# A graph layer with two expert choices per node: keys summed on VectorE, 16-bit marks of the choices' places, last rows stored in two pieces

## The chip, the cores and the metric

The kernel runs on one core of one Trainium2 chip. The metric is the device time of one execution in microseconds (us). TensorE (PE in the profile, PEld its weight loads), VectorE (DVE), ScalarE (ACT), GpSimd (POOL) and SyncE (SP, which here only issues transfers) run their own instruction streams side by side and wait for one another by semaphores. Matrix products end in PSUM, all other tiles lie in SBUF.

## The reference, cut to what matters

```python
xn = layernorm(x)                                    # x: [3125, 256]
# gnn: 53125 edges, sorted by dst
agg = segment_sum(edge_weight[:, None] * xn[src], dst, 3125);  gnn = agg @ W.T + b
# mix: linear attention, 8 heads
Q, K = elu(xn @ Wq) + 1, elu(xn @ Wk) + 1;  v = (xn @ Wv) / L
KV = einsum('nshd,nshv->nhdv', K, v)
Z = 1 / (einsum('nlhd,nhd->nlh', Q, K.sum(axis=1)) + 1e-6)      # the keys summed over tokens
mix = xn + layernorm(relu([xn, layernorm((Q KV Z L) @ Wm)] @ W1) @ W2)
x = x + gnn + mix
# ffn: 16 experts, the two best of each node, hidden size 512
n3 = layernorm(x);  top_probs, top_idx = top_k(softmax(n3 @ gate_w + gate_b), 2)
x = x + sum over the two choices of  gate * (silu(n3 @ w1[e]) * (n3 @ w2[e])) @ w3[e]
```

## The kernel before

The 3125 rows are 25 tiles of 128 tokens (NT = 25), of which the last has 53 rows (LAST). All is float32 but for a few bf16 marks. The stages follow each other:

1. **Load and normalise** (to about 42 us). x is loaded, normalised to xn, turned by TensorE, and the messages' rows y = xn @ W.T are made and stored to memory.
2. **Keys** (about 43 to 122 us). For t in 0..24 `project_k(t)` makes the key projection (L721); ScalarE (`exp_keys`, L417 and L419) and VectorE (`keys`, L1154) make the elu; three tiles later `sum_xk(t)` adds xn.T @ keys into one PSUM bank (L739) and, by a matmul of each key block with one column of ones (L742), the sum of the keys over the tokens into two columns of another. `xk_added` counts the tiles; GpSimd's gathers and SyncE's loads wait on it. Beside this the first two of 13 groups of edges are sorted: VectorE counts and places (`find_places`: L1054 to L1073, after TensorE's `prefix`, L683 to L686) and makes records (L1086, L1094), ScalarE makes one-hot marks of the slots (`slot_hot`, L382 and L384, four for each group), and TensorE puts a group in order by `reorder` (L695, 16 matmuls, four for each group). TensorE's order is written by hand: `reorder(0, k)` in tile steps 4, 6, 8 and 10, `prefix(1)` in step 17, `reorder(1, k)` in steps 22, 23, 25 and 27. ScalarE's: `slot_hot(0, k)` after tiles 1, 3, 5 and 7, `slot_hot(1, k)` after tiles 19, 20, 22 and 24. VectorE's is a list of `keys(first, end)` calls with the sort's parts between them. After the last `reorder`, `make_list(1)` (L1108 to L1132) and register loads on VectorE (`bins_named`) end the stage.
3. **Sums over edges** (about 124 to 840 us). 13 groups of 56 steps. GpSimd gathers 32 tiles of rows for each group (L633), ScalarE scales them, TensorE meets them with one-hot marks (L902, L912), VectorE adds into agg (L1212, L1218). The attention's and the next sort's parts are placed by hand beside the steps.
4. **Gate and routing** (about 840 to 922 us). n3 is made and stored (L313, and L314 for the last 53 rows), logits, the two choices, and for each choice its slot in the experts' list of 64 tiles (ETILES) of 128 places. `slots_ready` lets SyncE load the first experts' weights. Then the token of each place is found: VectorE marks the tile (`in_etile`, [P, 2, 25, 64] bf16) and the place in the tile (`in_place`, [P, 2, 25, 128] bf16) of each choice from int32 slots and a float32 iota (L1507), ScalarE multiplies `in_etile` by the row number (L559), GpSimd by the tile number (L645), and TensorE sums over tokens (L955). For each choice it waits for all three. VectorE turns the sums into token indices (L1511 to L1524, `tokens_ready`), GpSimd gathers the tokens' rows (L650).
5. **Experts** (about 926 to 1285 us). 64 tiles in a loop: 32 matmuls up (L978), 8 down (L988), three weight loads of 512 KB by SyncE for each, one gather and one scatter by GpSimd.
6. **End.** SyncE loads both choices' rows back, VectorE adds them with the gates, SyncE stores the output: four transfers of five tiles, one of four tiles (L361), one of the last 53 rows (L362), and waits for all.

## Time and profile before

| | |
|---|---|
| median of 3 runs | 1322.45 us (1321.16 to 1322.45) |
| the profiled execution | 1325.14 us, span in the profile 1323.4 us |
| busy PE / PEld / DVE / ACT / POOL | 1148.7 / 1016.0 / 850.8 / 537.1 / 621.3 us |
| mean granted TensorE clock | 0.939 of full |
| chain that ended last, by engine | PE 54%, DVE 21%, VectorE's queue 10%, issue 8%, ACT 3%, DMA 2% |

A busy share is an average over six stages with different limits. For each edit the row that counts is that of its own stage: who is waited for last there. The profiled execution is 1.7 us longer than its span and 2.7 us longer than the median.

### The profile page before, as it was taken

What the parts mean: (1) busy time and instruction counts of PE and PEld (TensorE: products, weight loads), DVE (VectorE), ACT (ScalarE), POOL (GpSimd) and SP (SyncE); (2) the same over time, 40 slices, a digit from 0 to 9 for tenths busy, and PEclk for the clock granted to TensorE, in tenths of its full rate; (3) what the DMA queues carried; (4) which work ended last, traced back from release to release, by engine and by line L of the source; (5) the groups of instructions that cost most, each with busy time, mean ns of one, the idle gap of its engine ahead of it and who ended that gap; (6) DMA issues with size and microseconds to landing.
All of it is one profiled execution on the core that took longest, in us unless ns stands there. A gap on an engine that the chain in (4) does not pass through costs nothing.

```text
span 1323.4 us, 21724 instructions
## 1 busy us (share of the span) xinstructions
PE 1148.7 (87%) x6831; PEld 1016.0 (77%) x6831; DVE 850.8 (64%) x1960; ACT 537.1 (41%) x1247; POOL 621.3 (47%) x624
## 2 busy tenths in 40 slices
PE   6998798999989899898998998741999999999980
PEld 5897686787868778687786886641999999999970
DVE  8644788888888888988889877857222222222226
ACT  4747575573856648466483742211011111111100
POOL 5845447566575755657566471004233333333320
PEclk9899899999999999999999999755999999999995
DMA  7213123222222222222222231205699999999948
GB/s 208 82 55 109 54 63 93 68 82 71 72 80 68 89 66 83 72 68 84 68 85 72 64 97 32 79 19 178 232 331 332 327 340 333 335 327 336 329 158 284
DMA packets 118372, 196.12 MB, mean 148 GB/s; under 512 B 13526, under 2 KB 67604, under 8 KB 118292
## 3 DMA queue, kind: packets, MB, share of 16 engines
q1 hardware_dynamic: 88958, 120.62, 27.5%
q0 software_dynamic: 26112, 71.34, 17.1%
q10 hardware_dynamic: 3222, 3.20, 0.7%
q8 instruction: 37, 0.61, 0.2%
q14 instruction: 43, 0.35, 0.1%
HBM read 177.12 MB, written 17.99 MB: 147 GB/s over the span
## 4 chain that ended last, share of the span: by engine, by line
PE 54%; DVE 21%; DVEq 10%; issue 8%; ACT 3%; DMA 2%; SPq 1%; ACTq 0%; POOL 0%; POOLq 0%
PE psum L978 17%; PE psum L988 8%; PE psum L902 6%; DVE agg L1212 5%; DVE agg L1218 4%; PE psum L912 3%; PE psum L721 3%; PE psum L695 3%; PE psum L789 2%; PE psum L739 2%; ACT in_slot L382 2%; PE psum L841 2%; DVE hot L1205 2%; DVEq L1297 1%; DVEq L1085 1%
## 5 line engine op out<-in xcount | busy, mean ns | idle before, releaser
L633 POOL DMA_INDIRECT arena<-y_rows,gather_i x416 | 440.6, 1059 | 301.6 <-PE psum L902 121.1
L902 PE MATMUL psum<-arena,hot 128*128 128x256 f32 x832 | 222.6, 397 | 15.9 <-DVE hot L1205 6.7
L1212 DVE TENSOR_TENSOR agg<-psum,agg 128x256 f32 x416 | 174.5, 420 | 44.8 <-DVE agg L1212 20.9
L479 ACT ACTIVATE arena<-arena,listed 128x256 f32<-128x256 f32 x416 | 175.6, 498 | 65.6 <-DMA arena<-y_rows,gather_i 65.5
L902 PEld LDWEIGHTS psum<-arena,hot 128*128 128x128 f32 x832 | 151.4, 195 | 53.1 <-issue 23.8
L978 PEld LDWEIGHTS psum<-arena 128*128 128x128 f32 x1536 | 181.4, 194 | 4.9 <-issue 2.5
L978 PE MATMUL psum<-arena 128*128 128x128 f32 x1536 | 181.9, 277 | 2.0 <-DVE arena L1531 2.0
L1538 DVE TENSOR_TENSOR arena<-psum,arena 128x512 f32<-128x512 f32 x64 | 44.3, 692 | 204.9 <-PE psum L978 204.9
L569 ACT ACTIVATE arena<-psum 128x512 f32<-128x512 f32 x64 | 38.3, 598 | 335.1 <-PE psum L978 335.1
L655 POOL DMA_INDIRECT chosen_rows<-arena,back_at x64 | 63.4, 990 | 219.7 <-DVE arena L1545 215.0
L382 ACT ACTIVATE in_slot<-iota,place_f 128x128 f32<-128x128 f32 x416 | 127.3, 390 | 62.2 <-DVE place_f L1073 62.0
L912 PE MATMUL psum<-arena,hot 128*128 x624 | 150.9, 382 | 1.5 <-DVE agg L1218 0.6
L912 PEld LDWEIGHTS psum<-arena,hot 128*128 128x128 f32 x624 | 115.5, 192 | 17.9 <-issue 3.7
L1218 DVE TENSOR_TENSOR agg<-psum,agg 128x512 f32<-128x512 f32 x156 | 106.0, 679 | 24.0 <-PE psum L912 22.4
L695 PE MATMUL psum<-record,in_slot 128*128 128x96 f32 x832 | 101.8, 275 | 0.0
L695 PEld LDWEIGHTS psum<-record,in_slot 128*128 128x128 f32 x832 | 99.5, 192 | 2.3
L988 PE MATMUL psum<-arena 128*128 128x256 f32 x384 | 90.8, 379 | 0.0
L650 POOL DMA_INDIRECT xnT<-n_rows,token_of x64 | 62.2, 972 | 28.4 <-issue 18.9
L988 PEld LDWEIGHTS psum<-arena 128*128 128x128 f32 x384 | 69.2, 190 | 7.4
L1094 DVE TENSOR_TENSOR record<-in_tile,edge 128x256 f32<-128x256 f32 x156 | 68.4, 447 | 5.5
L1545 DVE COPY arena<-psum 128x256 f32<-128x256 f32 x64 | 27.2, 425 | 60.7 <-PE psum L988 60.7
L1205 DVE TENSOR_TENSOR hot<-iota,node_in_bin 128x1024 f32<-128x1024 f32 x52 | 63.4, 1219 | 3.4 <-issue 2.5
(208 smaller groups left out, 1662.4 us busy)
## 6 DMA issues: line engine op xcount, KB each, us to landing
arena<-in_L_ffn_w_dram SPq DMA_DIRECT2D x144, 512.0 KB, 5.6
xnT<-in_L_ffn_w_dram SPq DMA_DIRECT2D x48, 512.0 KB
arena<-y_rows,gather_i POOLq DMA_INDIRECT x416, 2.8
arena<-chosen_rows SPq DMA_DIRECT2D x8, 640.0 KB, 8.9
y_rows<-w ACTq DMA_DIRECT2D x6, 512.0 KB, 2.9
agg<-in_x_dram SPq DMA_DIRECT2D x4, 640.0 KB, 6.7
n_rows<-arena SPq DMA_DIRECT2D x4, 640.0 KB
out_dram<-agg SPq DMA_DIRECT2D x4, 640.0 KB
```

The source lines that it names most:

```text
L382: act.activation(in_slot[k % 2][:, c, :], iota[:, :], ACT.Abs, bias=place_f[:, k * CH + c:k * CH + c + 1])
L479: last = act.activation(rows[h][:, t, :], rows[h][:, t, :], ACT.Copy, scale=weight[h][:, t:t + 1])
L633: pool.indirect_dma_start(rows[h][:, t, :], None, y_rows, bass.IndirectOffsetOnAxis(ap=gather_i[h][:, t:t + 1], axis=0)).then_inc(gathered ...
L695: last = pe.matmul(in_order, in_slot[k % 2][:, c, :], record[k % 2][:, c, :, :].rearrange("p f t -> p (f t)"), start=(k == 0 and c == 0), ...
L902: pe.matmul(bank_of(g, t // 2)[:, (t % 2) * C:(t % 2 + 1) * C], hot[:, n % HOTS, :], rows[h][:, t, :], start=True, stop=True).then_inc(met, 1)
L912: pe.matmul(bank_of(g, unit)[:, (b % 2) * C:(b % 2 + 1) * C], hot[:, n % HOTS, :], rows[h][:, bass.ds(row_of[b], 1), :].rearrange("p t c - ...
L978: last = pe.matmul(bank[b][:, m * P:(m + 1) * P], w[s][:, k * EH + m * P:k * EH + (m + 1) * P], e_xT[:, h, k * P:(k + 1) * P], start=(k == ...
L988: last = pe.matmul(bank[6 + h][:, 0:C], e_hid[:, h, k * P:(k + 1) * P], e_w3[s][:, k * C:(k + 1) * C], start=(k == 0), stop=(k == EHC - 1))
L1094: last = dve.tensor_tensor(record[k % 2][:, :, f, :], in_tile[:, :, :], edges_of(edge[:, f, :], g, k).unsqueeze(2).to_broadcast([P, CH, GT ...
L1205: dve.tensor_tensor(hot[:, n % HOTS:n % HOTS + BATCH, :], iota[:, :].unsqueeze(1).to_broadcast([P, BATCH, P]), of.unsqueeze(2).to_broadcas ...
L1212: dve.tensor_tensor(own, bank_of(g, t // 2)[:, (t % 2) * C:(t % 2 + 1) * C], own, ALU.add).then_inc(evicted, 1)
L1218: dve.tensor_tensor(own, bank_of(g, GT // 2 + a), own, ALU.add).then_inc(evicted, 1)
```

## The change

Four edits:

- The matmuls with ones leave `sum_xk`. VectorE adds each tile of keys to `keys_sum` ([P, 256] float32) instead: `sum_keys(t - 1)` comes right behind the key tile t, with a drain before it (26 instructions in all: a copy and 24 adds, with two of them behind the last tile). At the end of the keys stage TensorE waits for `keys_summed` and makes the two sums over partitions by one matmul each with ones. SyncE's load of Wm and W2, which overwrites the key tiles, waits for it as well.
- The slots' parts are copied to bf16, each value twice in a row (`slot_twice`, 200 elements from 100). The marks compare bf16 with bf16 (`iota_b`), in runs of two elements.
- GpSimd's multiplication by the tile number moves to VectorE (`number_tiles`), in the same form, between the marks: both `in_etile`, a drain, then for each choice the numbered tiles and `in_place`.
- The last 53 rows of n3 and of the output are stored as 48 rows and 5 rows.

```diff
+    ROUND = LAST // 16 * 16
...
                 for k in range(KC):
-                    pe.matmul(bank[5][:, k * C:(k + 1) * C], xn[0:tokens, t, k * P:(k + 1) * P], keys_of[0:tokens, t % 4, :],
-                              start=(t == 0 and k == 0), stop=(t == NT - 1), skip_group_check=True)
-                for m in range(KC):
-                    last = pe.matmul(bank[6][:, m:m + 1], keys_of[0:tokens, t % 4, m * P:(m + 1) * P], ones[0:tokens, 0:1],
-                                     start=(t == 0 and m == 0), stop=(t == NT - 1), skip_group_check=True)
+                    last = pe.matmul(bank[5][:, k * C:(k + 1) * C], xn[0:tokens, t, k * P:(k + 1) * P], keys_of[0:tokens, t % 4, :],
+                                     start=(t == 0 and k == 0), stop=(t == NT - 1), skip_group_check=True)
                 last.then_inc(xk_added, 1)
...
+            pe.wait_ge(keys_summed, 1)
+            for m in range(KC):
+                pe.matmul(bank[6][:, m:m + 1], keys_sum[:, m * P:(m + 1) * P], ones[:, 0:1], start=True, stop=True)
...
+            def sum_keys(t):
+                dve.drain()
+                if t == 0:
+                    return dve.tensor_copy(keys_sum[:, :], keys_of[:, 0, :])
+                n = P if t < NT - 1 else LAST
+                return dve.tensor_tensor(keys_sum[0:n, :], keys_sum[0:n, :], keys_of[0:n, t % 4, :], ALU.add)
...
                     dve.scalar_tensor_tensor(keys_of[:, t % 4, :], bank[t % 4][:, 0:C], 0.0, k_neg[:, t % KC, :], ALU.max, ALU.add).then_inc(k_ready, 1)
+                    if t >= 1:
+                        sum_keys(t - 1)
+                    if t == NT - 1:
+                        sum_keys(t).then_inc(keys_summed, 1)
...
-            for c in range(2):
-                pool.wait_ge(etiles_made, c + 1)
-                pool.tensor_tensor(numbered[:, c, :, 1, :], in_etile[:, c, :, :],
-                                   token[:, :, 1 + c].unsqueeze(2).to_broadcast([P, NT, ETILES]), ALU.mult).then_inc(tile_numbers, 1)
...
+            dve.tensor_copy(slot_twice[:, :, :, :, :].rearrange("p a c t b -> p (a c t) b"),
+                            slot_parts[:, :, :, :].rearrange("p a c t -> p (a c t)").unsqueeze(2).to_broadcast([P, 4 * NT, 2]))
+            dve.drain()
+            def by_twos(a, n):
+                return a.rearrange("p t (s b) -> p t s b", b=2), [P, NT, n // 2, 2]
+
+            def mark_choice(to, part, c, n, done):
+                to, whole = by_twos(to[:, c, :, :], n)
+                dve.tensor_tensor(to, slot_twice[:, part, c, :, :].unsqueeze(2).to_broadcast(whole),
+                                  iota_b[:, 0:n].rearrange("p (s b) -> p s b", b=2).unsqueeze(1).to_broadcast(whole), ALU.is_equal)\
+                    .then_inc(done, 1)
+
+            def number_tiles(c):
+                to, whole = by_twos(numbered[:, c, :, 1, :], ETILES)
+                dve.tensor_tensor(to, by_twos(in_etile[:, c, :, :], ETILES)[0], tile_twice[:, c, :, :].unsqueeze(2).to_broadcast(whole),
+                                  ALU.mult).then_inc(tile_numbers, 1)
+
+            for c in range(2):
+                mark_choice(in_etile, 1, c, ETILES, etiles_made)
+            dve.drain()
+            for c in range(2):
+                number_tiles(c)
+                mark_choice(in_place, 0, c, P, places_made)
...
-                    sp.dma_start(out[(NT - 1) * P:N, :], agg[0:LAST, NT - 1, :]).then_inc(out_written, 16)
+                    for first, end in ((0, ROUND), (ROUND, LAST)):
+                        sp.dma_start(out[(NT - 1) * P + first:(NT - 1) * P + end, :], agg[first:end, NT - 1, :]).then_inc(out_written, 16)
```

The store of n3's last rows (L314) is split in the same way, and the waits on `n3_stored` and `out_written` count one transfer more.

## Rows read from the trace of the kernel before

**Rows 1.** Windows: busy us (instructions) of each engine, then clock, DMA share, GB/s.
```profile
49.00:76.00 27.00, 27.00 (x156) 24.63 (x157) 13.66 (x26) 20.01 (x54) 11.06 (x15) 0.88 0.11 38
...
98.00:122.00 24.00, 24.00 (x162) 22.51 (x161) 9.82 (x32) 20.35 (x53) 17.49 (x19) 1.00 0.42 131
...
900.00:922.00 22.00, 5.91 (x50) 5.15 (x50) 17.48 (x14) 4.54 (x3) 11.15 (x3) 0.57 0.61 215
922.00:1285.00 363.00, 356.61 (x2688) 342.51 (x2688) 92.67 (x192) 38.28 (x64) 123.94 (x127) 0.99 0.91 310
```

**Rows 2.** Timeline of TensorE, one key tile: start us, us, instructions [idle before].
```profile
80.20 0.50 PE L742 MATMUL psum<-ones,w 128*128 128x1 f32 x4
...
80.56 1.11 PE L721 MATMUL psum<-wky,xnT 128*128 128x256 f32 x4
...
81.51 1.03 PE L739 MATMUL psum<-w,arena 128*128 128x256 f32 x4
...
82.37 0.50 PE L742 MATMUL psum<-ones,w 128*128 128x1 f32 x4
```

**Rows 3.** Timeline of ScalarE in the first sort, two waits for TensorE.
```profile
58.96 0.39 ACT L417 ACTIVATE wm<-psum 128x256 f32<-128x256 f32 x1 [1.01 <-PE psum L721]
...
65.09 0.39 ACT L417 ACTIVATE wm<-psum 128x256 f32<-128x256 f32 x1 [1.04 <-PE psum L721]
```

**Rows 4.** Timeline of the second sort, from its prefix to its list.
```profile
92.76 0.99 DVE L1054 SCALAR_TENSOR_TENSOR count<-psum,count 128x800 f32<-128x800 f32 x1 [0.59 <-PE psum L686]
...
97.27 2.46 ACT L382 ACTIVATE in_slot<-iota,place_f 128x128 f32<-128x128 f32 x8 [0.41 <-DVE place_f L1073]
...
114.14 1.06 ACT L384 ACTIVATE in_slot<-in_slot 128x1024 f32<-128x1024 f32 x1
...
117.75 2.02 PE L695 MATMUL psum<-record,in_slot 128*128 128x96 f32 x16
...
119.88 0.19 DVE L1108 CAST gather_i<-psum 128x32 int32<-128x32 f32 x1 [6.57 <-PE psum L695]
```

**Rows 5.** Timeline of VectorE, the same three instructions twice.
```profile
50.20 2.52 DVE L1094 TENSOR_TENSOR record<-in_tile,edge 128x256 f32<-128x256 f32 x3
...
60.88 1.10 DVE L1094 TENSOR_TENSOR record<-in_tile,edge 128x256 f32<-128x256 f32 x3
```

**Rows 6.** Timeline of GpSimd, first and last gather of group 0.
```profile
79.43 1.39 POOL L633 DMA_INDIRECT arena<-y_rows,gather_i  x1 [19.22 <-PE psum L742]
...
120.03 0.95 POOL L633 DMA_INDIRECT arena<-y_rows,gather_i  x1 [0.30 <-issue]
```

**Rows 7.** Timeline of the routing's last part.
```profile
900.17 3.56 DVE L1507 TENSOR_TENSOR xnT<-slot_parts,iota 128x1600 bf16<-128x1600 int32 x2
...
902.09 10.51 POOL L645 TENSOR_TENSOR xnT<-xnT,token 128x1600 bf16<-128x1600 bf16 x2 [99.69 <-DVE xnT L1507]
903.65 12.29 DVE L1507 TENSOR_TENSOR arena<-slot_parts,iota 128x3200 bf16<-128x3200 int32 x2
...
909.89 2.95 PE L955 MATMUL psum<-xnT,arena 128*128 128x128 bf16 x25 [20.08 <-DVE arena L1507]
...
916.00 2.95 PE L955 MATMUL psum<-xnT,arena 128*128 128x128 bf16 x25 [3.15 <-DVE arena L1507]
...
918.99 0.23 DVE L1511 TENSOR_SCALAR token_tile<-psum 128x64 f32<-128x64 f32 x1 [3.05 <-PE psum L955]
...
925.95 0.66 PE L966 MATMUL psum<-ident,xnT 128*128 128x128 f32 x2 [7.00 <-DMA xnT<-n_rows,token_of]
```

**Rows 8.** Chain of waits: 32 up matmuls of an early and a later expert tile.
```profile
927.32 6.34 PE psum L978 x32
935.12 3.81 PE psum L978 x32
```

**Rows 9.** Waits of SyncE: what for, us in total, times, longest.
```profile
SPq L317 <- DVEq L1499: 31.5, 1, 31.5
...
SPq L68 <- DMA out_dram<-agg: 5.2, 1, 5.2
```

**Rows 10.** End: issue of the last store; GB/s from 1285 us, in slices of 0.975 us.
```profile
1317.38 0.36 SPq L362 DMA_DIRECT2D out_dram<-agg  x1
...
GB/s 134 29 105 1 68 356 355 367 362 356 347 350 349 348 346 353 345 350 348 350 347 348 339 351 379 233 335 348 335 350 350 122 24 105 351 121 24 24 14 0
```

More of the change, by code:

```diff
@@ L303, in _ @@
             sp.wait_ge(xk_added, NT)
+            sp.wait_ge(keys_summed, 1)
             sp.dma_start(wm[:, :, :], Wm.rearrange(chunks, p=P)).then_inc(late_weights, 16)
@@ L313, in _ @@
                     sp.dma_start(n3_tiles[:, i * U:NT - 1, :], n3[:, i * U:NT - 1, :]).then_inc(n3_stored, 16)
[L314 removed]
+                    for first, end in ((0, ROUND), (ROUND, LAST)):
+                        sp.dma_start(n3_rows[(NT - 1) * P + first:(NT - 1) * P + end, :], n3[first:end, NT - 1, :]).then_inc(n3_stored, 16)
             def e_owner(q, s):
@@ L361, in _ @@
                     sp.dma_start(out_tiles[:, i * U:NT - 1, :], agg[:, i * U:NT - 1, :]).then_inc(out_written, 16)
-                    sp.dma_start(out[(NT - 1) * P:N, :], agg[0:LAST, NT - 1, :]).then_inc(out_written, 16)
-            sp.wait_ge(out_written, 16 * (TURNS + 1))
+                    for first, end in ((0, ROUND), (ROUND, LAST)):
+                        sp.dma_start(out[(NT - 1) * P + first:(NT - 1) * P + end, :], agg[first:end, NT - 1, :]).then_inc(out_written, 16)
+            sp.wait_ge(out_written, 16 * (TURNS + 2))
         @block.scalar
@@ L1504, in _ @@
             dve.drain()
-            for part, to, n, done in ((1, in_etile, ETILES, etiles_made), (0, in_place, P, places_made)):
-                for c in range(2):
-                    dve.tensor_tensor(to[:, c, :, :], slot_parts[:, part, c, :].unsqueeze(2).to_broadcast([P, NT, n]),
-                                      iota[:, 0:n].unsqueeze(1).to_broadcast([P, NT, n]), ALU.is_equal).then_inc(done, 1)
+            dve.tensor_copy(slot_twice[:, :, :, :, :].rearrange("p a c t b -> p (a c t) b"),
[18 more added lines that the diff above has]
+                mark_choice(in_place, 0, c, P, places_made)
             dve.wait_ge(tokens_summed, 1)
```

20 lines of the change are left out of this document (12 added, 8 removed).

## The prediction

> **What bounds the kernel now.** I read the page first (busy shares and the chain by line), then windows by stage, then the timeline of the stages that the diff touches, and for the end SyncE's waits and the transfers' rate. No single engine bounds the kernel, so each edit is costed in its own stage [rows 1]. In the keys stage TensorE is busy without a gap: 27.00 of 27.00 us and 24.00 of 24.00 us, VectorE only 13.66 and 9.82. ScalarE is the one to watch there, 20.35 of 24.00 us at the end of the stage. In the window of the routing's last part nothing but VectorE's marks is long: they run from 900.17 to 915.9 us and TensorE waits for them twice [rows 7]. The expert loop is TensorE's again, 356.61 of 363.00 us, with the transfers at a share of 0.91 close behind [rows 1]. At the end the program waits 5.2 us for the last store [rows 9]. Nothing in the diff touches the sums over edges or the expert loop, so a shift won ahead of them should pass through them whole, unless something that starts earlier now lacks its input; I come to that below.
>
> **The keys: what goes.** One tile takes TensorE 2.17 us, from 80.20 to 82.37 [rows 2]. The four matmuls with ones cost 0.36 us of it (80.20 to 80.56). The four of L721 behind them take 0.95 us to L739's start, where the four of L739, with as much work, take 0.86 (81.51 to 82.37): another 0.09 us goes with the weight loads for the short ones. I take 0.44 us for each tile. 25 tiles make 11.0 us; the first two ran at a lower clock (the window from 49 us has a mean of 0.88 [rows 1]), for which I add 0.5 us. TensorE alone would finish the stage 11.5 us earlier.
>
> **Does something else become the bound?** First sort: two tiles and one `reorder` make a period of 6.13 us (58.96 to 65.09), in which ScalarE idles 1.04 us [rows 3]. ScalarE's own work is thus 5.09 us, and TensorE's new period 6.13 - 0.88 = 5.25 us. TensorE stays the bound, just. 15 tiles' ones lie ahead of `prefix(1)`, so it comes 15 x 0.44 + 0.5 = 7.1 us earlier. Second sort: from here ScalarE sets the pace. `find_places` takes 4.51 us (92.76 to 97.27), and ScalarE's four `slot_hot` with the keys between them run without a gap from 97.27 to 114.14 + 1.06 = 115.20 us, 17.93 us [rows 4]. Before, TensorE came to the last `reorder` only at 117.75, 2.55 us after its marks. Now `find_places` starts at 92.76 - 7.1 = 85.7 us, plus 0.3 because the add behind key 17 stands in front of it and the prefix is now there sooner: 86.0. Then 86.0 + 4.5 + 17.9 + 0.1 of latency = 108.5 us for the last `reorder` against 117.75: 9.2 us. So of TensorE's 11.5 us some 2.3 stay behind a wait for ScalarE.
>
> **What VectorE's 26 instructions cost.** Three instructions of 256 elements take 1.10 us where GpSimd does not compute, 0.34 us from start to start with 0.08 us behind the last; beside GpSimd's adds, up to some 60 us, the same three take 2.52 us [rows 5]. With the drain I take 0.42 us each, 11 us in all, and up to 0.9 us each for the first four. VectorE has 13 us free in the first window and 14 in the last. They lie behind the key tile that TensorE waits for, but in front of the sort's records: two adds for each `make_records`, some 0.9 us. The first records were ready three to five us before their `reorder`, except the second set (made at 54 to 58 us, beside GpSimd's adds), where I expect the slack to be used up: 0.3 us lost. The whole edit is then worth 9.2 - 0.3 = **8.9 us**. Its bounds: 11.5 if ScalarE's run shrinks too; 4.5 if the adds also delay the records of the second sort by 0.9 us in each of four sets and the contended ones cost another 1 us. The two pairs of matmuls with ones at the end (0.4 us) and the wait for `keys_summed` (VectorE's last adds end about 1 us before the last `reorder`) stand behind that `reorder`, where TensorE has two us before the first marks of the sums are made; nothing for them. SyncE's load of Wm and W2 is queued behind the same wait, is needed some 20 us later, and comes earlier than before. If the adds' cover were gone, they would cost their 11 us and eat the gain.
>
> **The shift's inputs.** GpSimd's 32 gathers of group 0 run back to back from 79.43 to about 121 us [rows 6], and their first waits for tile 9, which comes 4 us earlier. They end near 117 us, while the sums now begin near 115 instead of 124. The sums take their tiles in order over 55 us, and the first four tiles are there by 84 us, so this holds. Group 1's first gather slips to 117 from the 113 it could have had; it has 50 us. Nothing lost.
>
> **The marks.** Two instructions of 1600 elements start at 900.17 and leave the engine to the next at 903.65: 1.74 us each [rows 7]. With 0.34 us for 256 elements [rows 5] that is 0.07 us and 1.04 ns for each element; 3200 elements should take 3.41 us. They took 6.1 (903.65 to 915.94 for two), while GpSimd's multiplication stood beside them, itself 5.3 us for 1600 elements [rows 7]. So the marks of the places and GpSimd hold each other up, and moving the multiplication ends that. What the 16-bit form costs no row shows. From above it is 1.04 ns an element, as 32-bit operands; from below nothing but 0.07 us an instruction. I take half, 0.52 ns: the row's operands are four bytes wide, the new ones two and adjacent, so the same bytes for each ns. Then 1600 elements take 0.90 us, 3200 take 1.74.
>
> The Trainium skill (VectorE: DVE Perf Modes, "Mode 2×_1P — pack two bf16 into one 32-bit read") says that a two-source instruction handles two elements in a cycle if all operands are 16 bits wide with step 1. By it the estimate is the same 0.52 ns. Its page Vector Engine (DVE) Microarchitecture Reference, 5.1, adds that a single element read again and again by step 0 ran one at a time, a row read again did not; no run here shows either yet.
>
> New order, from 900.17: the copy to `slot_twice` (200 elements, 0.07 + 0.21 and its end, 0.35) and a drain, marks begin at 900.6. Two `in_etile` to 902.5 with the drain, number 0 to 903.4, place 0 to 905.2, number 1 to 906.1, place 1 to 907.9. ScalarE's rows' numbers (1.7 us each) are done by then. TensorE's sums for choice 0 take 2.95 us for 25 matmuls [rows 7], from 905.3 to 908.3, those for choice 1 follow at once, to 911.3: TensorE ends this, not VectorE. VectorE reads the sums at 911.3 against 918.99: **7.7 us**. At 1.04 ns an element the same list ends with place 1 at 914.7 and the sums at 917.7: 1.3 us. At the lower bound TensorE's 5.9 us remain, behind a first mark near 901: 11 us. The experts' first three weight sets are loaded from 900.4 on and need some 14 us, so the first tokens now come while the third is still in flight; only the first is needed. Behind that the gather of tokens took 4.5 us already with loads in flight, and the fourth set is issued earlier by the same 7.7 us.
>
> **The last rows.** For n3 the store has 31.5 us until `slots_ready` [rows 9]: nothing. At the output the rate falls from 351 to 24 GB/s for the last 2.5 us [rows 10]: one stream of the sixteen carries 53 rows, 54 KB, 2.3 us at 24 GB/s. As 48 and 5 rows the first piece spreads. One issue more (0.4 us) stands beside data in flight. Bounds: 2.8 us, and -0.4 if the pieces don't spread. I take **2.3 us**.
>
> **Sum.** 8.9 + 7.7 + 2.3 = 18.9 us. The profiled execution of 1325.14 us (span 1323.4) becomes 1306.2; it stood 2.7 us above the median, so the median becomes 1322.45 - 18.9 = 1303.5 us.
>
> **Rivals.**
>
> 1. *The 16-bit marks are no faster for each element.* For it: no 16-bit row of VectorE with two inputs in this trace. Against: the operands' bytes halve. The edit gives 1.3 us in place of 7.7: 1309.9.
> 2. *The keys' gain is cut by ScalarE and the sort.* For it: ScalarE has only 1.04 us a period and 2.55 us at the end [rows 3, 4], and each add stands in front of a record. Against: VectorE's free half. At the bound of 4.5 us: 1307.9.
> 3. *The two pieces don't spread*, which is that this edit doesn't do what it says: 1303.5 + 2.7 = 1306.2.
> 4. *Slower: TensorE's clock stays low into the experts.* At 900 to 922 us it is granted 0.57 [rows 1], so near the lower of its levels (1.2 of 2.4 GHz), and the first tile's 32 up matmuls took 6.34 us where the next took 3.81 [rows 8]. If the two sums now run together and the pause ahead of the experts ends in another state, each tile at the low level costs 5.5 us more (its 5.5 us doubled); four such tiles eat the whole gain, six make it 14 us slower, 1336. Against it: the same pause of 7 us [rows 7] stays, with the same work on both sides, and the clock came back within one tile.
>
> **Chances and range.** My forecast 0.60, rival 1 0.14, rival 2 0.15, rival 3 0.05, rival 4 0.03, and 0.03 that several losses leave no change. A measurement of this kernel tells about 0.2% (2.6 us) from no change; all cases but the last two lie further below, so faster 0.94, same 0.03, slower 0.03. The forecast's own range is 1300.5 to 1306.5 (ScalarE's run and the marks' start to either side). For 8 in 10 it has to reach down to 1299.5 (keys at 11.5 and marks somewhat better) and up past rival 1: 1311.
>
> **What the profile would show.** No L742-like matmuls between the keys, one tile every 1.73 us in the middle of the stage, ScalarE without idle in the second sort and TensorE waiting for it before the last two `reorder`s; the last `reorder` near 108.5 us and the first sum near 116.5. Two marks of 3200 elements in 1.8 us each, and no pause between the two runs of 25 matmuls. No slices of 24 GB/s at the end. The prediction is wrong if VectorE's adds run long beside GpSimd, if the keys stage still ends above 112 us, or if the marks take more than 3 us.

## The result, and the profile after

The changed kernel takes 1306.17 us (median of 4, 1305.15 to 1307.45), the kernel before 1322.45 us (median of 4, 1321.16 to 1322.8). The ratio is 0.988, interval 0.9864 to 0.9896: faster, inside the range, 2.7 us above the predicted 1303.5. The profiled execution takes 1306.58 us; 1306.2 was forecast for it. One execution of wide_marks (1518.81 us) and one of after_again (1391.16 us), both below, ran in a slower state of the chip, at a mean granted clock of 0.73 and 0.82, so they stand in the medians given there but not in the ratios.

The windows of the kernel after: busy us (instructions) of PE, PEld, DVE, ACT and POOL, then granted clock, DMA share, GB/s.

```profile
49.00:76.00 27.00, 27.00 (x150) 23.83 (x149) 22.13 (x50) 21.25 (x58) 14.24 (x17) 0.94 0.08 30
98.00:122.00 24.00, 17.45 (x94) 14.13 (x94) 13.76 (x45) 16.46 (x39) 17.27 (x18) 0.84 0.44 138
...
912.00:1270.00 358.00, 354.70 (x2681) 341.04 (x2680) 92.25 (x191) 38.21 (x64) 120.47 (x123) 0.99 0.90 309
```

Against [rows 1], VectorE went from 13.66 to 22.13 us in the first window and TensorE stayed full. At the stage's end TensorE now idles, since the stage ends at 109 us instead of 120. The expert loop is as it was.

The timeline of TensorE, VectorE and ScalarE in the keys stage, for [rows 2, 4 and 5]: start us, us, instruction [idle before].

```profile
53.20 2.02 PE L698 MATMUL psum<-record,in_slot 128*128 128x96 f32 x16
...
55.21 2.54 DVE L1097 TENSOR_TENSOR record<-in_tile,edge 128x256 f32<-128x256 f32 x3
...
74.26 1.03 PE L724 MATMUL psum<-wky,xnT 128*128 128x256 f32 x4
75.13 1.03 PE L742 MATMUL psum<-w,arena 128*128 128x256 f32 x4
75.99 0.27 PE L705 MATMUL psum<-ident,listed 128*32 128x128 f32 x1
...
84.63 0.98 DVE L1057 SCALAR_TENSOR_TENSOR count<-psum,count 128x800 f32<-128x800 f32 x1
...
89.13 2.45 ACT L390 ACTIVATE in_slot<-iota,place_f 128x128 f32<-128x128 f32 x8 [1.13 <-DVE place_f L1076]
...
102.04 2.00 PE L698 MATMUL psum<-record,in_slot 128*128 128x96 f32 x16 [0.35 <-ACT in_slot L392]
...
105.81 1.06 ACT L392 ACTIVATE in_slot<-in_slot 128x1024 f32<-128x1024 f32 x1
...
107.01 2.00 PE L698 MATMUL psum<-record,in_slot 128*128 128x96 f32 x16 [0.16 <-ACT in_slot L392]
```

A key tile takes 1.73 us (74.26 to 75.99) where it took 2.17. ScalarE's run of slot marks is 106.87 - 89.13 = 17.7 us (forecast 17.9), TensorE waits for it ahead of the last two `reorder`s, and the last one starts 10.7 us earlier than in [rows 4]: 107.01. In VectorE's groups by line, the 24 adds L1157 take 432 ns each, the forecast's 0.42 us. With the one copy (L1155) they are 25 instructions; the 26 of the change's description, of the prediction and of the expectations is one too many, which is 0.4 us of VectorE's time and changes no reading.

The timeline of the routing's last part, for [rows 7], with the first tiles of the experts, for [rows 8].

```profile
891.34 0.27 DVE L1519 CAST slot_twice<-slot_parts 128x200 bf16<-128x200 int32 x1
...
891.68 1.89 DVE L1527 TENSOR_TENSOR xnT<-slot_twice,iota_b 128x1600 bf16<-128x1600 bf16 x2
...
893.67 0.99 DVE L1533 TENSOR_TENSOR xnT<-xnT,tile_twice 128x1600 bf16<-128x1600 bf16 x1
894.58 1.82 DVE L1527 TENSOR_TENSOR arena<-slot_twice,iota_b 128x3200 bf16<-128x3200 bf16 x1
...
896.46 4.53 PE L958 MATMUL psum<-xnT,arena 128*128 128x128 bf16 x50 [15.46 <-DVE arena L1527]
897.22 1.82 DVE L1527 TENSOR_TENSOR arena<-slot_twice,iota_b 128x3200 bf16<-128x3200 bf16 x1
...
901.02 0.23 DVE L1544 TENSOR_SCALAR token_tile<-psum 128x64 f32<-128x64 f32 x1 [1.98 <-PE psum L958]
...
903.38 0.94 POOL L653 DMA_INDIRECT xnT<-n_rows,token_of  x1 [108.97 <-DVEq L1558]
...
909.16 0.66 PE L969 MATMUL psum<-ident,xnT 128*128 128x128 f32 x2 [8.18 <-DMA xnT<-n_rows,token_of]
...
910.53 6.55 PE L981 MATMUL psum<-arena 128*128 128x128 f32 x32 [0.71 <-DVE arena L1564]
...
918.54 3.81 PE L981 MATMUL psum<-arena 128*128 128x128 f32 x32 [1.24 <-DVE arena L1564]
```

3200 marks take 1.82 us where they took 6.1; both choices' 50 matmuls are one run. The sums are read 10.0 us behind the slots' parts instead of 19.2. Behind that, the tokens' gather needs until 909.1, 5.7 us from its issue, where it took 4.5. The up matmuls are as in [rows 8], so rival 4 did not occur.

SyncE's waits in the kernel after, for [rows 9]: waited for, us in total, times, longest.

```profile
SPq L324 <- DVEq L1513: 33.9, 1, 33.9
...
SPq L69 <- DMA out_dram<-agg: 2.3, 1, 2.3
```

Milestones of the two profiled executions, in us from the start of the span, and what each step gave:

| | before | after | gained here |
|---|---|---|---|
| first sum of products (L739, L742) | 48.96 | 48.39 | 0.6 |
| first `reorder` | 56.01 | 53.20 | 2.2 |
| last `reorder` of group 1 | 117.75 | 107.01 | 7.9 |
| gate's prefix | 888.78 | 879.96 | -1.9 |
| slots' parts | 899.82 | 890.99 | 0.0 |
| sums read | 918.99 | 901.02 | 9.1 |
| first tile's matmuls | 925.95 | 909.16 | -1.2 |
| first load back | 1287.85 | 1271.28 | -0.2 |
| end of span | 1323.4 | 1304.7 | 2.1 |

The last column adds up to 18.6 us, the difference of the two spans (18.7) up to rounding; the forecast was 18.9. A profile of another execution of the same kernel (after_again, below) splits this otherwise: routing 8.1 and -1.0, for example, in place of 9.1 and -1.2.

### The profile page after: what moved, and what is told of

It reads as the page before. It is cut to its first block, busy times and chain, and to the rows that moved or that the text cites. A ratio compares the mean times of both kernels' runs of the same rounds, so it can differ in the third digit from the quotient of the medians.

```text
span 1304.7 us, 21589 instructions
## 1 busy us (share of the span) xinstructions
PE 1135.4 (87%) x6735; PEld 1003.3 (77%) x6735; DVE 852.6 (65%) x1988; ACT 534.8 (41%) x1247; POOL 615.7 (47%) x623
## 4 chain that ended last, share of the span: by engine, by line
PE 51%; DVE 21%; DVEq 11%; issue 9%; ACT 4%; DMA 2%; SPq 1%; ACTq 1%; POOL 0%; POOLq 0%
PE psum L981 18%; PE psum L991 8%; DVE agg L1226 5%; PE psum L905 5%; DVE agg L1232 4%; PE psum L915 3%; PE psum L724 3%; ACT in_slot L390 2%; PE psum L698 2%; PE psum L792 2%; DVE hot L1219 2%; PE psum L844 1%; DVEq L1311 1%; DVEq L1072 1%; DVEq L1088 1%
```

## The experiments

The first four kernels ran together, against 1322.17 us before (median of 21 executions).

**keys_only**: the kernel before with the keys' edit alone.

```diff
                 for k in range(KC):
...
-                for m in range(KC):
-                    last = pe.matmul(bank[6][:, m:m + 1], keys_of[0:tokens, t % 4, m * P:(m + 1) * P], ones[0:tokens, 0:1],
...
+                        sum_keys(t - 1)
```

> The kernel before with the keys edit alone: the matmuls with ones leave the key tiles, VectorE adds the keys. The trace of the changed kernel has its last reorder of the second sort at 107.0 us (117.75 before), yet stands only 8.8 us ahead at the gate's prefix (888.78 against 879.96). My theory: this edit alone gives 9 to 10.5 us, some 1311.5 to 1313.5 against a median of 1322.45, and the last reorder starts at 107 to 108 us. Rival, that the sums over edges give part of the shift back every time: 7 to 8 us, 1315. Rival, that ScalarE's run bounds it as I wrote on record: last reorder at 108.5 us.

1314.84 us, ratio 0.9953 (0.9940 to 0.9967). First `reorder` at 53.05, last at 106.85, gate's prefix at 877.26. By the medians that is 7.3 us, less than the 9 to 10.5 of the theory and in the range of the first rival, but not for the rival's reason: in the trace nothing is given back, the lead over the kernel before is 10.9 us at the last `reorder` and 11.5 us at the gate. 3.0 us of it are there at the first `reorder` already, and routing_only below has its first `reorder` just as early without the edit: they come from TensorE's clock in the profiled executions.

**adds_only**: VectorE's 25 instructions are added and nothing is taken away; TensorE still makes the sums with ones and does not read `keys_sum`.

```diff
+                    if t >= 1:
+                        sum_keys(t - 1)
+                    if t == NT - 1:
+                        sum_keys(t).then_inc(keys_summed, 1)
```

> The kernel before, which keeps all its matmuls with ones, and has VectorE's copy and adds of the keys besides (their sum is used by nothing). It prices the 26 instructions alone. My theory, that they lie in VectorE's free time while TensorE sets the pace: within 0.5 us of before, last reorder at 117.5 to 118.3 us. Rival, that they stand in front of the records and cost part of the gain: 1 to 4 us slower than before, with TensorE idle ahead of a reorder. At full price, with no cover, 11 us slower.

1323.38 us, ratio 1.0007 (0.9998 to 1.0016). First `reorder` 56.13, last 117.88, each 0.1 us later than before. The medians lie 1.2 us apart, but the interval holds 1. While TensorE has its old work, the adds are covered: of their 11 us the trace shows 0.1, and the interval allows at most 2.

**rows_only**: the two stores of 53 rows alone are split into 48 and 5.

```diff
-                    sp.dma_start(out[(NT - 1) * P:N, :], agg[0:LAST, NT - 1, :]).then_inc(out_written, 16)
+                    for first, end in ((0, ROUND), (ROUND, LAST)):
+                        sp.dma_start(out[(NT - 1) * P + first:(NT - 1) * P + end, :], agg[first:end, NT - 1, :]).then_inc(out_written, 16)
```

> The kernel before with the last 53 rows of n3 and of the output stored as 48 and 5 rows. On record: 2.3 us faster, bounds 2.8 and -0.4. SyncE's wait for the last store falls from 5.2 to 2.3 us in the changed kernel's trace, with 0.4 us more of issue ahead of it: 1.9 to 2.5 us, 1320.0 to 1320.5. Rival, that the store of n3 matters too: more than 3 us. Rival, that part of it is execution to execution: under 1 us.

1319.57 us, ratio 0.9989 (0.9980 to 0.9998). From the first load back to the end of the span it takes 1319.4 - 1286.0 = 33.4 us, before 35.55. SyncE's waits show the pieces spread:

```profile
SPq L69 <- DMA out_dram<-agg: 2.3, 1, 2.3
```

**routing_only**: the changed kernel with the keys' edit and the split stores undone.

```diff
-                        sum_keys(t - 1)
...
-                    for first, end in ((0, ROUND), (ROUND, LAST)):
```

> The kernel before with the routing edit alone (16-bit marks with the slot twice, tile numbers on VectorE). In the changed kernel's trace the sums are read 9.1 us earlier counted from the parting of the slots, of which the first gather of the experts' tokens gives 1.2 us back (5.6 us in place of 4.5). On record: 7.7 us. My theory: 7.5 to 8 us, 1314.5 to 1315, the two runs of 25 matmuls joined. Rival, that a gather beside the weights' loads gives more back: 5 to 6 us. The three parts should add up to the whole, 16.3 us by the medians and 18.6 by the two profiled executions; if they add up to 18 to 19, the median of the whole was unlucky or the parts get in each other's way.

1315.07 us, ratio 0.9952 (0.9938 to 0.9965). Slots' parts to sums read 10.06 us, from there to the first tile 8.24, so 7.8 us of the 26.1 between the slots' parts and the first tile are gone, as forecast. By the medians the keys are worth 7.3 us, the rows 2.6 and the routing 7.1, together 17.0 where the whole gave 16.3. By the ratios on record, which are not the quotients of these medians, the parts make 0.47 + 0.11 + 0.48 = 1.06%, the whole 1.2% here and 1.11% in a second set of runs (after_again, below). They add up within their intervals.

This run also has the old keys stage and yet starts its first `reorder` at 53.05 us, 3 us before that of the kernel before. The windows of the first microseconds of the stage, in the kernel before:

```profile
49.00:56.00 7.00, 7.00 (x22) 5.87 (x22) 6.07 (x10) 6.80 (x21) 7.00 (x10) 0.54 0.43 143
```

routing_only:

```profile
49.00:56.00 7.00, 6.82 (x43) 6.28 (x44) 6.09 (x10) 6.77 (x20) 7.00 (x10) 1.00 0.40 143
```

and the changed kernel:

```profile
49.00:56.00 7.00, 7.00 (x34) 5.66 (x33) 6.52 (x12) 6.73 (x20) 7.00 (x9) 0.76 0.29 108
```

The granted clock is 0.54 (near the lower level, 1.2 GHz), 1.00 (2.4 GHz) and 0.76. It differs with the execution: adds_only, with VectorE's adds as the one difference, repeats the kernel before (0.54), rows_only, with no change at all in this stage, has 0.76 and its first `reorder` at 54.66. With the clock up, the first `reorder` comes at 53.05 both with the matmuls with ones (routing_only) and without them (keys_only). So in that state the ones ahead of it are worth nothing. In the changed kernel TensorE's preparation for it waits for the records:

```profile
52.86 0.29 PEld L696 LDWEIGHTS psum<-meets,ones 25*128 25x128 f32 x2 [0.55 <-DVE record L1097]
```

From the first to the last `reorder`, routing_only and keys_only differ by 61.75 - 53.80 = 7.95 us, before and after by 61.74 - 53.81 = 7.93. A third pair is rows_only (116.40 at the last `reorder`) and the changed kernel, both at 0.76 in that window: 9.4 us at the last `reorder`, of which 1.5 at the first, 0.7 of that with the start of the stage (49.07 against 48.39).

The next four ran on another chip, where the kernel before took 1336.94 us (median of 7; why is taken up at the end). The changed kernel was not run there. What is used of them is their routing stage and, of adds_twice, the start of its keys stage; the changed kernel's own numbers are those above.

**marks_single**: the marks and numbers are the same, in bf16, but each slot is one element, read again by step 0.

```diff
-                dve.tensor_tensor(to, slot_twice[:, part, c, :, :].unsqueeze(2).to_broadcast(whole),
-                                  iota_b[:, 0:n].rearrange("p (s b) -> p s b", b=2).unsqueeze(1).to_broadcast(whole), ALU.is_equal)\
+                dve.tensor_tensor(to[:, c, :, :], slot_twice[:, part, c, :, 0].unsqueeze(2).to_broadcast([P, NT, n]),
+                                  iota_b[:, 0:n].unsqueeze(1).to_broadcast([P, NT, n]), ALU.is_equal)\
...
```

> The changed kernel, with the 16-bit slot, tile number and iota read as single elements: the slot and the tile number are broadcast one element at a time (step 0) in place of runs of two. Same types, same results. If the pairs are what makes the marks fast, 3200 elements take 3.4 us in place of 1.82 and 1600 take 1.75 in place of 0.99, and the sums are read at about 16 us from the parting of the slots in place of 10.0: 5 to 6 us slower than the changed kernel, 1311 to 1312.5. If 16 bits alone do it, nothing changes: 1306.

Ratio 0.9932 (0.9915 to 0.9949), 1328.0 us. Slots' parts to sums read 17.77 us; the expectation's 16 was too low, the prediction's own list for marks at 1.04 ns an element (917.7 - 899.8 = 17.9) was right. Its timeline:

```profile
906.83 3.56 DVE L1526 TENSOR_TENSOR xnT<-slot_twice,iota_b 128x1600 bf16<-128x1600 bf16 x2
...
910.48 1.82 DVE L1531 TENSOR_TENSOR xnT<-xnT,tile_twice 128x1600 bf16<-128x1600 bf16 x1
912.22 3.49 DVE L1526 TENSOR_TENSOR arena<-slot_twice,iota_b 128x3200 bf16<-128x3200 bf16 x1
```

The time is that of 32-bit operands again: 3.56 us for two marks of 1600 elements, as in [rows 7], and 3.49 for one of 3200, where wide_marks (below) takes 3.48. The multiplication takes 1.82 us where it took 0.99 in pairs. Two bytes an operand are not enough; the pair is what halves it. The Trainium skill says as much (Vector Engine (DVE) Microarchitecture Reference, 5.1: one element read 16 times by step 0 ran one at a time); the trace agrees, 3.49 us for 3200 marks against 1.82 in pairs.

**gpsimd_numbers**: the 16-bit pairs stay, the multiplication goes back to GpSimd.

```diff
+            for c in range(2):
+                pool.wait_ge(etiles_made, c + 1)
+                pool.tensor_tensor(numbered[:, c, :, 1, :], in_etile[:, c, :, :],
+                                   token[:, :, 1 + c].unsqueeze(2).to_broadcast([P, NT, ETILES]), ALU.mult).then_inc(tile_numbers, 1)
...
-                number_tiles(c)
```

> The changed kernel, but GpSimd multiplies by the tile number as before, beside the 16-bit marks. My theory: GpSimd and a VectorE instruction with two inputs in SBUF hold each other up, so its two multiplications end the stage: 3 to 5 us each, the second done some 8 to 10 us after the first marks, the sums read 12 to 14 us from the parting of the slots (10.0 in the changed kernel): 1308 to 1311. Rival, that the marks are short enough not to meet it: GpSimd 3 us each, the sums read within 1.5 us of the changed kernel's.

1323.43 us, ratio 0.9889 (0.9867 to 0.9911). Slots' parts to sums read 14.52 us, where 12 to 14 were expected. The stage is 4.5 us longer than the changed kernel's, though its ratio lies beside that kernel's two (0.988 and 0.9889), which were measured elsewhere: across chips the ratios don't tell these kernels apart. Its timeline:

```profile
909.91 8.00 POOL L654 TENSOR_TENSOR xnT<-xnT,token 128x1600 bf16<-128x1600 bf16 x2 [102.65 <-DVE xnT L1532]
910.64 8.95 DVE L1532 TENSOR_TENSOR arena<-slot_twice,iota_b 128x3200 bf16<-128x3200 bf16 x2
```

The marks of 3200 elements take 4.5 us each beside GpSimd, 1.82 without it, and GpSimd's multiplication 4.0 us instead of 5.3 beside the slower marks: each holds the other up. What VectorE loses to the two multiplications is the same with both forms of the marks: 8.95 - 2 x 1.82 = 5.3 us here, 12.29 - 2 x 3.48 = 5.3 us in [rows 7] (3.48 from wide_marks). That would fit instructions that take turns whole, with 2.7 us for a multiplication by itself; this is an estimate, since no run has GpSimd's multiplication without marks beside it.

**wide_marks**: int32 slots and float32 iota as before, but VectorE numbers the tiles.

```diff
-                dve.tensor_tensor(to, slot_twice[:, part, c, :, :].unsqueeze(2).to_broadcast(whole),
...
+                dve.tensor_tensor(to[:, c, :, :], slot_parts[:, part, c, :].unsqueeze(2).to_broadcast([P, NT, n]),
...
+                dve.tensor_tensor(numbered[:, c, :, 1, :], in_etile[:, c, :, :],
+                                  token[:, :, 1 + c].unsqueeze(2).to_broadcast([P, NT, ETILES]), ALU.mult).then_inc(tile_numbers, 1)
```

> The changed kernel with the marks of before (int32 slots against a float32 iota) but the tile numbers on VectorE, from a float32 tile number. It shows the move alone. By the rates on record: 1.74 + 1.82 for the tiles, then 1.74 and 3.41 us for each choice: place 1 ends 14.2 us after the first mark, the sums are read at 17.5 us from the parting of the slots, against 19.2 before and 10.0 in the changed kernel. So the move alone gives 1.5 to 2 us of the 9.1 and the two-byte pairs the rest: 1312.5 to 1314. Rival, that the marks of the places are slow for another reason than GpSimd: 6.1 us each still.

1329.52 us, ratio 0.9940 (0.9920 to 0.9960). Slots' parts to sums read 17.36 us, against 19.17 before: moving the multiplication alone gives 1.8 us, as expected. That is no more than 0.4 us better than marks_single, so 16 bits without the pairs gain nothing. Its marks, with GpSimd idle:

```profile
913.10 3.48 DVE L1520 TENSOR_TENSOR arena<-slot_parts,iota 128x3200 bf16<-128x3200 int32 x1
```

**adds_twice**: each tile of keys is added twice, to `keys_sum` and to a second sum that nobody reads.

```diff
             def sum_keys(t):
                 dve.drain()
...
+                    dve.tensor_tensor(keys_sum2[0:m, :], keys_sum2[0:m, :], keys_of[0:m, t % 4, :], ALU.add)
+                dve.drain()
```

> The changed kernel with each of the 26 instructions that sum the keys made twice, the second into a tile that nothing reads. The kernel before with the adds alone was 0.9 us slower. My theory: here TensorE has less to hide them, and ScalarE's run starts behind an add: last reorder 0.5 to 2 us later than 107.0, 1306.5 to 1308.5. Rival, that VectorE's work in the keys stage is free altogether: within 0.5 us. Rival, that it is nearly the bound: more than 4 us slower than the changed kernel.

1323.59 us, ratio 0.9904 (0.9887 to 0.9921). Its timeline of VectorE beside GpSimd's adds (which run to 61.7 us):

```profile
56.33 0.44 DVE L1159 TENSOR_TENSOR keys_sum<-keys_sum,w 128x256 f32<-128x256 f32 x1
56.84 0.79 DVE L1164 TENSOR_TENSOR keys_sum<-keys_sum,w 128x256 f32<-128x256 f32 x1
```

The first add takes 0.44 us even beside GpSimd, the second 0.79. From the start of the sums of products to the first `reorder` it takes 54.55 - 49.30 = 5.25 us; in profiles with single adds and the clock up there it takes 4.5 to 4.95 (keys_only, gpsimd_numbers, back_split). So the doubled adds cost 0.3 to 0.7 us there. From the first to the fourth `reorder` they cost nothing that shows: 72.02 - 54.55 = 17.5 us, as in back_split, gpsimd_numbers and warm_split, where the adds are single. All four are 1.7 us longer there than the changed kernel, for a reason that back_split shows below. The cover was thin: the second records were ready at 61.1 us, TensorE came to them at 61.54. What the doubled adds cost behind that this run can't tell, since engines stood still from 102 to 111 us on this chip. So neither the theory (0.5 to 2 us at the last `reorder`) nor its rivals are settled.

The last four ran together, against 1322.4 us before (median of 9).

**after_again**: the changed kernel itself without any edit, to have a second profile of it.

> The changed kernel as it is, so that the kernels of this group have it beside them on the same chip, and a second profiled execution of it. The three parts alone gave 7.3, 7.1 and 2.6 us by their medians. My theory, that the parts add up: a ratio to the kernel before of 0.986 to 0.989. Rival, that the first ratio was lucky or unlucky: outside that. In the trace the first reorder of the keys stage starts at about 53 us if TensorE's clock is up by then and at 55 to 56 us if not, which alone moves the span by up to 3 us.

1307.9 us, ratio 0.9889 (0.9873 to 0.9905), as expected. First `reorder` at 53.08, last at 106.87. The sums are read 11.1 us behind the slots' parts, 1.0 later than in the first profile (its 50 matmuls take 5.57 us, not 4.53), and the first tile comes 7.9 us behind that. The first eight matmuls of the sums take 1.97 us, where the first profile of the same kernel has 3.75:

```profile
115.68 1.97 PE L905 MATMUL psum<-arena,hot 128*128 128x256 f32 x8 [0.42 <-DVE hot L1219]
```

From the last `reorder` to the gate's prefix it takes 771.1 us, the first profile 772.95, the kernel before 771.03.

**back_split**: three more transfers of 53 rows (a load of x, both choices' rows at the end) split into 48 and 5.

```diff
-                        sp.dma_start(to[0:LAST, whole, :], chosen_rows[first:first + LAST, :]).then_inc(chosen_back[i], 16)
+                        for a, b in ((0, ROUND), (ROUND, LAST)):
+                            sp.dma_start(to[a:b, whole, :], chosen_rows[first + a:first + b, :]).then_inc(chosen_back[i], 16)
```

> The changed kernel with three more transfers of 53 rows in two pieces of 48 and 5: the last rows of x at the start, and those of both choices' rows loaded back at the end. VectorE waits 1.9 us for the last rows back, behind 24 GB/s for 2 us. My theory: the same cure as for the store gives 1.5 to 2.5 us more there, and nothing at the start: 0.1 to 0.2% below the changed kernel. Rival, that the loads before it in the queue set the end and the single stream runs beside them: under 0.5 us.

1303.56 us, ratio 0.9858 (0.9842 to 0.9874): some 0.3% (4 us) below after_again, more than the 0.1 to 0.2% of the theory. From the first load back to the end 30.9 us, the changed kernel 33.4: the 2.5 us that the trace shows for the edit, at the upper end of the theory. What gives the rest is open. The end in the changed kernel:

```profile
1295.95 4.21 DVE L1607 SCALAR_TENSOR_TENSOR agg<-arena,gates,agg 128x256 f32<-128x256 f32 x10 [1.88 <-DMA arena<-chosen_rows]
```

In back_split VectorE goes through all 50 without that wait:

```profile
1277.53 20.70 DVE L1609 SCALAR_TENSOR_TENSOR agg<-arena,gates,agg 128x256 f32<-128x256 f32 x50 [9.01 <-DMA arena<-chosen_rows]
```

Its last `reorder` comes 2.8 us later (109.80). 1.1 us of that is there at the first `reorder` (the first sum of products starts 1.0 us later, 49.38); the split load of x is not the reason, since warm_split has it and starts at 48.20, and adds_twice starts at 49.30 without it. The other 1.7 us come between the first and the second `reorder`, 61.33 - 54.33 = 7.0 us apart where the changed kernel has 58.54 - 53.20 = 5.3, and there TensorE waits for nobody. It runs slower:

```profile
54.33 3.03 PE L700 MATMUL psum<-record,in_slot 128*128 128x96 f32 x16
57.15 1.75 PE L726 MATMUL psum<-wky,xnT 128*128 128x256 f32 x4
...
61.33 1.92 PE L700 MATMUL psum<-record,in_slot 128*128 128x96 f32 x16
```

The window from 55 to 58 us, first in back_split, then in the changed kernel:

```profile
55.00:58.00 3.00, 3.00 (x15) 2.88 (x14) 2.76 (x5) 2.87 (x8) 2.86 (x5) 0.52 0.02 5
55.00:58.00 3.00, 3.00 (x17) 2.67 (x16) 2.93 (x5) 2.80 (x7) 2.86 (x4) 1.00 0.00 0
```

The granted clock is 0.52 against 1.00. VectorE's second records are no part of it: they take 2.5 us beside GpSimd in both kernels (56.63 to 59.15 here, 55.21 to 57.75 there). In gpsimd_numbers, adds_twice and warm_split the same window has 0.57, 0.50 and 0.63, and the same 7.0 us between the first two `reorder`s. So in the changed kernel a low stretch ahead of the first `reorder` is hidden behind the records (53.20 and 53.08 us in its two profiles, 53.05 with the clock up in keys_only), and one that falls behind it costs 1.7 us.

**warm**: matmuls whose result nobody reads fill TensorE's pauses, 6 behind the first key tiles, 5 ahead of the first sum over edges, 8 ahead of the routing's sums and 14 behind them.

```diff
+                    pe.matmul(bank[b][:, first:first + C], ident[:, :], wv[:, 0, :], start=True, stop=True)
...
+            for _ in range(8):
+                pe.matmul(bank[5][:, 0:C], ident[:, :], wq[:, 0, :], start=True, stop=True)
```

> The changed kernel with idle stretches of TensorE filled by float32 matmuls whose result nothing reads: 6 in the keys stage before the first sum of products, 5 before the first sum over edges, 8 while VectorE marks the choices and 14 while the experts' first tokens are gathered. If the low clock of TensorE behind a pause costs what the rows say (the first expert tile 6.55 us in place of 3.8, the first eight matmuls of the sums 3.75 in place of 2.45, up to 3 us in the keys stage, 0.5 at the tokens' sums), this gives 3 to 7 us: 0.25 to 0.5% below the changed kernel, and the scatter of the keys stage goes. Rival, that each of these stretches waits for something else anyway (records, gathers, weights): under 1 us. Rival, that the filling matmuls run into the work behind them: slower than the changed kernel.

1303.5 us, ratio 0.9850 (0.9832 to 0.9869): some 0.4% (4 to 5 us) below after_again, within the 3 to 7 us of the theory. The first expert tile's up matmuls take 3.81 us (changed kernel 6.55, after_again 5.62), and from the first tile to the first load back it takes 359.2 us instead of 362.1 (after_again 361.2). The five ahead of the sums cost here: the first sum comes 10.4 us behind the last `reorder`, in after_again, with the same low clock behind that `reorder`, 8.8. In warm_split, with the clock up there, they cost nothing: 7.9 us as in the changed kernel. The theory's word that the scatter of the keys stage goes was not borne out: the executions of warm still run from 1299.42 to 1304.67 us, and in warm_split, with the same six matmuls, the clock falls behind the first `reorder` all the same.

**warm_split**: both edits.

```diff
+            keep_warm(3, 0, 5)
...
+                        for a, b in ((0, ROUND), (ROUND, LAST)):
```

> Both additions at once, as the candidate that beats both kernels. They lie in different stages, so their gains should add: 0.4 to 0.7% below the changed kernel, a ratio to the kernel before of 0.981 to 0.984.

1298.98 us (1297.72 to 1302.74), ratio 0.9834 (0.9814 to 0.9854): the fastest, 0.6% below after_again by the ratios, as expected, with no overlap of the executions' ranges (after_again from 1304.62). TensorE at the routing:

```profile
889.85 5.50 PE L961 MATMUL psum<-wq,ident 128*128 128x256 f32 x16 [9.96 <-DVEq L1524]
895.35 1.67 PE L967 MATMUL psum<-xnT,arena 128*128 128x128 bf16 x25
897.99 1.67 PE L967 MATMUL psum<-xnT,arena 128*128 128x128 bf16 x25 [0.96 <-DVE arena L1538]
...
908.46 3.81 PE L992 MATMUL psum<-arena 128*128 128x128 f32 x32 [0.71 <-DVE arena L1575]
```

25 matmuls take 1.67 us instead of [rows 7]'s 2.95, and TensorE waits again for VectorE's marks between the choices.

## Why the prediction was right, step by step

**The keys.** Forecast 9.2 us at the last `reorder`, less 0.3; measured 10.7, and 7.95 between two executions whose clock and first `reorder` agree. Within the stage the steps held almost to the tenth: the ones ahead of the first `reorder` were put at 2 x 0.44 + 0.5 = 1.4 us, so from the first to the last the forecast is 9.2 - 1.4 = 7.8 us, and both pairs show 7.9. `find_places`' start (84.63, forecast 86.0), ScalarE's run (17.7, forecast 17.9) and ScalarE as the one waited for at the end are all there. The step that was mis-sized is the head: 1.4 us there holds only while the clock is low. With the clock up, TensorE waits for the first records and the ones' cost is hidden; that is worth 0. In the profiled pair the head gave 2.8 us, since the execution of before had a clock of 0.54 and that of after 0.76. The 1.4 us thus hold for some executions only.

The adds' price was right (0.43 us); beside GpSimd's adds they cost no more, where up to 0.9 was allowed. What VectorE would lose at the second records was put at 0.3 us. It was 0 in every profile with the keys' edit: TensorE comes to the second `reorder` without a wait. The 1.7 us that back_split, gpsimd_numbers, warm_split and adds_twice lose there are TensorE's own, at the lower clock, a case that the prediction has no term for. Rival 2, the keys cut to 4.5 us, did not occur.

**What the sums gave back.** On the way from the last `reorder` to the gate the profiled execution lost 1.9 us, so 8.8 us arrive where 8.9 were forecast. Against after_again, the same kernel, it lost 1.84 us. That is no single place. The first sum's eight matmuls take 3.75 us against 1.97 (the granted clock from 114 to 124 us is 0.51 in the one and 0.84 in the other), but after_again has its low clock just ahead of them. Counted from the last `reorder`, VectorE's same instructions lie 1.84 us apart at 39 us, 0.17 at 107, 1.85 at 164 and 0.17 at 281, and 1.8 us again from 614 us on, which stays to the gate. There the granted clock falls in the first profile alone; first its window, then after_again's, then VectorE's wait for TensorE in the first:

```profile
718.00:722.00 4.00, 4.00 (x13) 3.21 (x12) 2.49 (x8) 3.93 (x11) 2.02 (x3) 0.57 0.21 66
718.00:722.00 4.00, 4.00 (x22) 3.32 (x22) 3.78 (x10) 3.93 (x11) 2.88 (x3) 1.00 0.32 98
721.60 0.42 DVE L1226 TENSOR_TENSOR agg<-psum,agg 128x256 f32 x1 [1.33 <-PE psum L905]
```

So a low stretch in the sums costs 1.7 us where TensorE is the one waited for, and whether an execution has one more or one less of them at the end of the sums is its luck. That 8.8 us arrive where 8.9 were forecast is luck too: 1.8 too little at the `reorder`, 1.9 lost behind it, which the second profile of the same kernel does not lose.

**The routing.** Forecast 7.7 us, measured 9.1 - 1.2 = 7.9; 7.8 in routing_only and 7.1 in after_again (11.1 + 7.9 us against 26.1). The marks are right: 0.52 ns an element, 0.99 and 1.82 us for 0.90 and 1.74, TensorE last. Rival 1 was rightly priced too: with single elements, marks_single's stage to the first tile takes 17.77 + 6.89 = 24.7 us against 26.1 before, 1.5 us gained where the rival said 1.3. Of the 8 us, the move off GpSimd and the pairs need each other: the move alone gives 1.8 us (wide_marks), the pairs beside GpSimd 19.17 - 14.52 = 4.7 (gpsimd_numbers), both 9.1. Two terms were off and cancel in part. TensorE's 50 matmuls took 4.5 us for 5.9; the granted clock from 896 to 901 us is 0.68, so it came up in their midst (after_again 5.57). And "the gather of tokens took 4.5 us already with loads in flight" gave no price to the third set of weights still in flight: 1.2 us are given back, in the changed kernel and in routing_only (8.14 and 8.24 us from the sums to the first tile, 6.96 before). The windows of that gather, in the kernel before:

```profile
921.40:925.90 4.50, 0.00 (x0) 0.00 (x0) 0.00 (x0) 0.00 (x0) 3.58 (x4) 0.61 0.70 223
```

and in the changed kernel:

```profile
903.40:909.00 5.60, 0.00 (x0) 0.00 (x0) 0.00 (x0) 0.00 (x0) 3.76 (x4) 0.74 1.07 373
```

The transfers' share is 1.07 instead of 0.70: the gather shares full DMA engines. The seven profiles that read the sums 9.8 to 11.1 us behind the slots' parts need 7.6 to 8.2 us from there to the first tile, the seven that read them from 14.5 us on need 6.9 to 7.1. That fits the third set of weights, but no run held the loads back to prove it.

**The last rows.** Forecast 2.3 us, measured 2.1, and SyncE's last wait 5.2 to 2.3. Rival 3 did not occur. What the argument passed over is that the same slow stream carried 53 rows in three more transfers, two of them on the same path: 2.5 us more (back_split).

**The point.** The sum, 18.9 us, met the pair of profiled executions (18.56). The median fell by 16.3. The base was the median and the terms came from one execution 2.7 us above it, while that of after stands 0.4 above its own: 18.56 - 2.7 + 0.4 = 16.3. So the step that put the forecast 2.7 us too low is the last one, which took a sum read from a slow profile off the median without asking what made that profile slow. Executions of the kernel before run from 1319.45 to 1325.14, and part of that is TensorE's clock, with up to 3 us at the start of the keys and 1.7 us for a low stretch elsewhere. That the sum met the profiled pair within 0.3 us is in part luck: the head and the sums' loss cancel. How the last 1 or 2 us split among the three edits stays open: neither the medians nor the ratios tell that.

## What to carry to other kernels

Price each edit in its own stage and ask which engine ends that stage afterwards: here ScalarE's marks took over in the keys and TensorE's sums in the routing, and naming them beforehand gave each stage's gain within a microsecond where the clock was the same. Take the base and the terms from the same execution, or say what sets them apart. For the comparison and the multiplication here, 16-bit values paid on VectorE only with the innermost two elements of every operand side by side (1.82 against 3.49 us), so store a value that is broadcast twice in a row; and don't put GpSimd's multiplication beside it (4.5 us). When a transfer of an odd number of rows turns up once at 24 GB/s, look for all its sisters, and before a term is read from two profiles, check the granted clock in both, at the head of the stage and within it: a wait that seems to move may be TensorE itself at half its clock.

## What the runs showed of the hardware

- The same instructions at the start of the keys stage got a clock of 0.54, 0.76 or 1.00 in different executions, which moves the first `reorder` by 3 us where the matmuls with ones lie ahead of it (56.01, 54.66, 53.05) and by 0.2 us in keys_only and the changed kernel, where they don't (53.05, 53.08, 53.20).
- VectorE and GpSimd hold each other up by kind of instruction: marks of 3200 elements went from 1.82 to 4.5 us, three records' instructions from 1.10 to 2.53, but a single add of 256 elements stayed at 0.44 and only the one right behind it took 0.79. With two forms of the marks VectorE loses the same 5.3 us to GpSimd's two multiplications.
- On the other chip, each of the four profiles has waits of VectorE or ScalarE of 4 to 9 us between 88 and 122 us that the profile puts down to no instruction of the program (`remote` or `issue`). None of the other ten profiles has one above 3.5 us there. The longest, in adds_twice, by ScalarE's timeline:

```profile
101.80 0.42 ACT L428 ACTIVATE wm<-wm 128x256 f32<-128x256 f32 x1
111.61 2.44 ACT L391 ACTIVATE in_slot<-iota,place_f 128x128 f32<-128x128 f32 x8 [9.40 <-remote]
```

The wait is for nothing that the profile names (VectorE waits there as well, 6.76 us), and the kernel before was 14.5 us slower there than on the chip of the last four runs. No experiment was made on its cause, so it stays open.
